# Five columns of gathers taken off GpSimd and fetched row by row by ScalarE and SyncE, with first transfers, last chunk and last wait moved

## The chip, the cores and the metric

One core of one Trainium2 chip. The metric is the device time of the kernel in microseconds, the median of several executions. The kernel is written out by hand: one instruction stream for each engine, with semaphores between them, in four blocks that follow one another.

## What is computed

Two layers of a graph network over 12,500 nodes and 412,500 edges with 64 features; the edges are sorted by their target node dst. Cut to what matters:

```python
edge_index_t = jnp.stack([src, dst], axis=1)
h = jnp.maximum(_layernorm(x), 0.0)
# layer 0: gated MLP of every edge, summed at dst
m = silu(silu(edge @ W1 + b1) @ W2 + b2) * sigmoid(silu(edge @ G1 + g1) @ G2 + g2)
x = x + h + segment_sum(m, dst, n)
# layer 1: attention over the edges of each node
h = jnp.maximum(_layernorm(x), 0.0)
se, re = (h @ Ws + bs)[src], (h @ Wr + br)[dst]
logits = einsum('ehd,d->eh', mish(se + re), aw) + ab
ex = exp(logits - segment_max(logits, dst)[dst])
out = segment_sum(ex / segment_sum(ex, dst)[dst] * se, dst)
x = x + out
```

## The kernel before

**Edge stage** (`edge_mlp`, 202 chunks of 2 x 1024 edges). SyncE loads the edges with features on the partitions (`load`, line 277), TensorE and ScalarE run the gated MLP, VectorE multiplies and forms running sums along the edges with a scan (line 490) that a keep mask restarts at each new node; TensorE turns the sums into rows, and SyncE stores every running sum in DRAM (`sums`). The mask `keep16` comes from comparing neighbours in dst (line 559). It goes to DRAM and comes back spread over partitions (`load_keep`, line 281). A search, spread over the chunks and fed by samples of dst (lines 321 to 335), finds for each node its last edge (`R["last"]`, `R["end"]`) and its first (`R["start"]`), 98 columns of 128 nodes. In program order SyncE issues: edges 0, three pieces of dst, edges 1, the samples, edges 2 and 3, then waits for the mask. ScalarE issues all the first weights (lines 448 to 459). GpSimd's last act is to load x into `R["base"]` in seven pieces (line 667).

**Node update** (`update_nodes`). GpSimd gathers the sum of each node's last edge, 98 indirect DMAs of 128 rows (line 754), one for each column, then scatters 98 columns of projected rows back into `sums` (line 760), a group of seven columns at a time when VectorE has it ready (`sr_ready`). The 14 groups run through: VectorE `center` (line 820), ScalarE Square and Sqrt (`root`, lines 789 and 791), VectorE `scale`, TensorE transposes (777), ScalarE's two copies to `hT` (806), TensorE's projection (782), VectorE's addition to `sr` (846). There are four `sr` buffers; group k waits until the scatters of group k - 4 have landed. On VectorE `project(k - 1)` stands ahead of `spread_of(k)`; on ScalarE `root(k + 1)` stands behind the copies of group k.

**Attention** (`attention`, 135 chunks of up to 24 edges on each of 128 partitions; the last two have 16). GpSimd gathers the senders' rows, a column of 128 at a time (1044). Some columns are not gathered by it: SyncE (line 1000) and ScalarE (line 1112) read node numbers from SBUF into registers (`reg_load`, lines 997 and 1109) and issue one direct DMA for each row. ScalarE computes mish in four activations: Tanh (1081), Square (1087), Ln (1089) and Exp (1095), the last two with a table load each, and the Exp goes to PSUM, where it must wait until the copy of the previous chunk's states (`arows`, line 1156) has left it. VectorE forms the logits (1217 to 1219), the running maximum and the weighted sums by scans. SyncE stores the running states of every edge (`states`, line 984) and waits at the end until all have landed (line 1032).

**Finish** (`finish`). A short chain over VectorE, TensorE and ScalarE joins the states across partitions, GpSimd reads and writes back the rows concerned (1340, 1342), and then gathers the final state of each node, 98 indirect DMAs of 128 rows of 72 values (1347), seven for a group. VectorE divides and adds (1419 to 1427), SyncE stores (1333). Two buffers q; a group waits until the one two before it has been taken.

## Time and profile before

| | us |
|---|---|
| median of 3 runs | 5454.18 (5453.94 to 5455.4) |
| the profiled execution | 5462.94, its span 5461.1 |
| edge stage, node update, attention, finish (start of each) | 0, 1091.0, 1341.2, 5318.3 |
| busy, share of the span | GpSimd 66%, VectorE 79%, ScalarE 53%, TensorE 20% |
| DMA, mean over the span | 115 GB/s; 262 GB/s in most of the edge stage |

Times are microseconds from the start of the span. Busy shares are averages over stages with different limits, so each change is to be read in its own stage. "Idle before, releaser" in square brackets is how long the engine had stood idle before an instruction and what ended that; "issue" means that nothing in the profile held it but its own instruction stream. A name like SPq or ACTq is the queue of an engine, which issues DMAs.

### The profile page before, as it was taken

Reading aid. Unit: us, or ns where it says so; the run is one execution under the profiler, and the core shown is the slowest. Engines: PE = TensorE matmul, PEld = TensorE weight load, DVE = VectorE, ACT = ScalarE, POOL = GpSimd, SP = SyncE. Lnnn points to the kernel's source line nnn. Section 1 sums busy time; section 2 is a strip of 40 time slices with the busy share of each in tenths; the row PEclk is TensorE's granted clock in tenths of the full one; section 3 lists DMA queues with packets and bytes.
Section 4 is the critical chain, followed back from the end, with each engine's and each line's share of the span. In section 5 each row is a group of like instructions: output and inputs, shape, how many; then the busy total and the mean of one; then the engine's idle time right before and its main releaser. Section 6 shows DMA issues by size and latency. Waiting matters only on the chain. (4 is left out here: it accounts for less than half of the span.)

```text
span 5461.1 us, 64454 instructions
## 1 busy us (share of the span) xinstructions
PE 1117.6 (20%) x8383; PEld 509.2 (9%) x8383; DVE 4320.5 (79%) x4065; ACT 2889.7 (53%) x3445; POOL 3594.0 (66%) x3683
## 2 busy tenths in 40 slices
PE   8999999913000000000000000000000000000000
PEld 3444444412000000000000000000000000000000
DVE  7999988753698888888888888888888888888881
ACT  7999999811355445444444444454454454454440
POOL 2444420077777777777777777777777777777757
PEclk9999999955555555555555555555555555555555
DMA  8888888721232333332332332332332332333322
GB/s 229 263 262 262 265 261 266 234 47 58 64 101 77 88 89 78 88 89 77 89 89 76 89 89 77 89 89 76 89 88 77 89 88 78 89 84 81 86 58 50
DMA packets 326140, 630.21 MB, mean 115 GB/s; under 512 B 126683, under 2 KB 130292, under 8 KB 325550
## 3 DMA queue, kind: packets, MB, share of 16 engines
q1 hardware_dynamic: 200862, 501.41, 28.3%
q0 software_dynamic: 117904, 125.12, 12.2%
q14 instruction: 328, 2.69, 0.2%
q10 hardware_dynamic: 7040, 0.89, 0.1%
q8 instruction: 6, 0.10, 0.0%
HBM read 391.97 MB, written 235.04 MB: 115 GB/s over the span
## 5 line engine op out<-in xcount | busy, mean ns | idle before, releaser
L1044 POOL DMA_INDIRECT se<-s_proj,idx x2053 | 1942.2, 946 | 626.3 <-issue 626.0
L1044 POOL DMA_INDIRECT r_se<-s_proj,idx x1026 | 970.7, 946 | 313.1 <-issue 313.1
L1134 ACT ACTIVATE held_ps<-exin 128x96 f32<-128x96 f32 x135 | 34.2, 254 | 1920.5 <-DVE z L1206 1914.7
L1354 PE MATMUL a_ps<-r_ident,r_state 128*4 128x128 f32 x1 | 0.4, 373 | 4001.9 <-DVE drop L1383 4001.9
L490 DVE TENSOR_TENSOR_SCAN sums<-keepb,sums,msg 128x1024 f32<-128x1024 bf16 x201 | 472.6, 2351 | 31.3 <-DVE msg L481 27.4
L1245 DVE TENSOR_TENSOR_SCAN work_ps<-work_ps,wse 128x1632 f32<-128x1632 f32 x135 | 479.1, 3549 | 4.6
L419 ACT ACTIVATE hidden<-h_ps,r_b1g 128x1024 f32<-128x1024 f32 x404 | 460.2, 1139 | 4.6 <-PE h_ps L363 4.6
L1192 DVE TENSOR_TENSOR_SCAN held_ps<-held_ps,rnew 128x1536 f32<-128x1536 f32 x135 | 452.2, 3350 | 4.6
L1206 DVE TENSOR_TENSOR z<-se,held_ps 128x1536 f32<-128x1536 f32 (+1 forms) x90 | 244.9, 2721 | 254.6 <-DMA se<-s_proj,idx 241.1
L374 PE MATMUL v_ps<-hidden,r_w2g 64*64 64x512 f32 x1616 | 438.5, 610 | 17.2 <-issue 1.9
L375 PE MATMUL g_ps<-hidden,r_w2g 64*64 64x512 f32 x1616 | 438.5, 616 | 0.0
L363 PE MATMUL h_ps<-edges,r_w1g 64*64 64x512 f32 x3232 | 433.3, 594 | 20.3 <-DMA r_w1g<-in_L_gnn_G 16.4
L1185 DVE SCALAR_TENSOR_TENSOR rnew<-held_ps,rs 128x1536 f32<-128x1536 f32 x135 | 373.6, 2767 | 60.1 <-DVE nlast L1247 42.2
L630 POOL DMA_INDIRECT nodes<-in_dst,block x102 | 167.4, 1641 | 367.1 <-DVE block L521 335.9
L1354 PEld LDWEIGHTS a_ps<-r_ident,r_state 128*4 128x4 f32 x1 | 0.1, 81 | 4002.2 <-DVE drop L1383 4002.2
L426 ACT ACTIVATE value<-v_ps,b 128x512 f32<-128x512 f32 x404 | 281.6, 697 | 61.6 <-PE v_ps L374 56.1
L1217 DVE SCALAR_TENSOR_TENSOR work_ps<-work_ps,z 128x1536 f32<-128x1536 f32 x135 | 236.1, 1749 | 97.6 <-issue 64.1
L481 DVE SCALAR_TENSOR_TENSOR msg<-gate,value 128x1024 f32<-128x1024 f32 x202 | 246.4, 1220 | 77.5 <-ACT gate L429 76.2
L385 PE MATMUL tr_ps<-r_ident,sums 128*128 128x128 f32 x1616 | 287.5, 301 | 5.2 <-DVE rows L497 4.6
L429 ACT ACTIVATE gate<-g_ps,g 128x512 f32<-128x512 f32 x404 | 281.8, 698 | 0.0
L1156 ACT ACTIVATE arows<-work_ps 128x1632 f32<-128x1632 f32 x135 | 205.5, 1522 | 129.3 <-issue 125.3
L1238 DVE TENSOR_TENSOR wse<-se,held_ps 128x1536 f32<-128x1536 f32 (+1 forms) x90 | 248.7, 2763 | 3.1
(210 smaller groups left out, 4650.4 us busy)
## 6 DMA issues: line engine op xcount, KB each, us to landing
states<-arows SPq DMA_DIRECT2D x133, 864.0 KB
edges<-in_edge_attr SPq DMA_DIRECT2D x202, 512.0 KB, 4.8
sums<-rows SPq DMA_DIRECT2D x402, 256.0 KB
rs<-sums SPq DMA_DIRECT2D x133, 768.0 KB, 5.2
fetched<-s_proj SPq DMA_DIRECT2D x6304, 0.2 KB
keepb<-keep SPq DMA_DIRECT2D x404, 128.0 KB, 3.8
fetched<-s_proj ACTq DMA_DIRECT2D x3040, 0.2 KB
se<-s_proj,idx POOLq DMA_INDIRECT x2053
```

Source lines behind the costliest of these rows:

```text
L363: last = nc.tensor.matmul(h_ps[u][units, s, :], R["w1g1"][feats, units], edges[m][feats, half], start=True, stop=True)
L374: last_v = nc.tensor.matmul(v_ps[out, :], R["w2g2"][0:F, :], hid[0:F, s, :], start=True, stop=True)
L375: last_g = nc.tensor.matmul(g_ps[out, :], R["w2g2"][F:2 * F, :], hid[F:2 * F, s, :], start=True, stop=True)
L385: last = nc.tensor.transpose(tr_ps[:, k, j * P:(j + 1) * P], cols[:, 4 * k + j, :], R["ident"][:, :])
L419: nc.scalar.activation(hidden[u][:, :, :], h_ps[u][:, :, :], ACT.Silu, bias=R["b1g1"][:, :]).then_inc(hidden_ready, 1)
L426: nc.scalar.activation(value[m][:, half], v_ps[:, :], ACT.Silu, bias=b2[:, :]).then_inc(gated, 1)
L429: nc.scalar.activation(gate[m][:, half], g_ps[:, :], ACT.Tanh, scale=0.5, bias=g2[:, :]).then_inc(gated, 1)
L490: nc.vector.tensor_tensor_scan(sums[m][:, :], keepb[m][:, :], msg[m % 2][:, :], carry, ALU.mult, ALU.add).then_inc(scanned, 1)
L1044: pool.indirect_dma_start(out=se[b][:, k, :], out_offset=None, in_=D["s_proj"], in_offset=bass.IndirectOffsetOnAxis(ap=node[:, k:k + 1], a ...
L1185: nc.vector.scalar_tensor_tensor(new, hold, 1.0, rs[b][:, 0:w, :].rearrange("p k f -> p f k"), ALU.subtract, ALU.mult).then_inc(rnew_ready, 1)
L1192: nc.vector.tensor_tensor_scan(held_ps[:, 0:F * w], held_ps[:, 0:F * w], flat(new), 0.0, ALU.mult, ALU.add)\
L1245: do(nc.vector.tensor_tensor_scan(work_ps[:, 0:H * HE * w], work_ps[:, 0:H * HE * w], sums.rearrange("p h e t -> p (h e t)"), 0.0, ALU.mul ...
```

## The change

- Node update: GpSimd gathers 96 columns in place of 98. ScalarE fetches the rows of the last two: 16 pieces (`fetch`) of one register load and 16 direct DMAs each, two pieces behind `root(k + 1)` in each of the steps k = 0 to 7. The last group waits for them. VectorE multiplies the row numbers to byte offsets first.
- Finish: 95 columns gathered in place of 98. Of the last three, ScalarE fetches one (eight pieces, one for each of the first eight groups) and SyncE two (16 pieces), into a buffer of their own. ScalarE takes over the stores of the output from SyncE.
- The five columns of row numbers reach the issuing engines' layout through DRAM: GpSimd writes them (five DMAs) and reads them back (one) at the end of the edge stage.
- First transfers: the second weights and biases are issued by SyncE behind edges 0, no longer by ScalarE. SyncE then waits for all the weights before it issues edges 1 and 2 and only then dst.
- Last chunk of the attention: its Tanh and Square move ahead of the exponentials of the chunk before, its Exp writes to SBUF in place of PSUM and stands ahead of the copy to `arows`; VectorE adds its senders right behind the reduction of the logits.
- Last wait: SyncE no longer waits for the stores of states at the end of the attention; GpSimd does at the start of the finish. Buffers and semaphores outlive the block for that.

```diff
             load(0, 0)
+            sp.dma_start(R["w2g2"][0:F, :], A["L0_gnn_W2"]).then_inc(weights_in, 16)
+            sp.dma_start(R["w2g2"][F:2 * F, :], A["L0_gnn_G2"]).then_inc(weights_in, 16)
+            for k in range(2):
+                rows_k = slice(F * k, F * k + F)
+                sp.dma_start(b2[rows_k, :], column(A["L0_gnn_b2"]), **one).then_inc(weights_in, 16)
+                sp.dma_start(g2[rows_k, :], column(A["L0_gnn_g2"]), **one).then_inc(weights_in, 16)
+            sp.wait_ge(first_in, 16 * FIRST_WEIGHTS)
+            sp.wait_ge(weights_in, 16 * WEIGHTS)
+            load(1, 1)
+            load(2, 2)
...
-            load(1, 1)
...
-            load(2, 2)
...
-            act.dma_start(R["w2g2"][0:F, :], A["L0_gnn_W2"]).then_inc(weights_in, 16)
-            act.dma_start(R["w2g2"][F:2 * F, :], A["L0_gnn_G2"]).then_inc(weights_in, 16)
-            for k in range(2):
-                rows_k = slice(F * k, F * k + F)
-                act.dma_start(b2[rows_k, :], column(A["L0_gnn_b2"]), **slow).then_inc(weights_in, 16)
-                act.dma_start(g2[rows_k, :], column(A["L0_gnn_g2"]), **slow).then_inc(weights_in, 16)
...
-            pool.wait_ge(x_in, 16 * (NS // 2))
+            pool.wait_ge(chain, LAST_KNOWN)
+            for i in range(FAR_LAST + FAR_END):
+                of = R["last"][:, NJ - FAR_LAST + i:NJ - FAR_LAST + i + 1] if i < FAR_LAST else R["end"][:, NJ - FAR_END - FAR_LAST + i:NJ - FAR_END - FAR_LAST + i + 1]
+                pool.dma_start(column(D["far"][i * P:(i + 1) * P]), of, **slow).then_inc(x_in, 16)
+            pool.wait_ge(x_in, 16 * (NS // 2 + FAR_LAST + FAR_END))
+            pool.dma_start(R["far"][:, :, :], D["far"].rearrange("(i g q) -> g i q", g=P // GANG, q=GANG), **slow).then_inc(x_in, 16)
+            pool.wait_ge(x_in, 16 * (NS // 2 + FAR_LAST + FAR_END + 1))
...
         def _(pool):
-            for j in range(NJ):
+            for j in range(NJ - FAR_LAST):
...
+            def fetch(i, g):
...
+                rows_at = [act.alloc_register(f"last_{i}_{g}_{q}") for q in range(GANG)]
+                act.reg_load(rows_at, R["far"][g:g + 1, i, :])
+                for q in range(GANG):
+                    at = act.snap(rows_at[q], donate=True, min_val=0, max_val=(P * RUN - 1) * 4 * F)
+                    act.dma_start(agg[g * GANG + q:g * GANG + q + 1, NJ - FAR_LAST + i, :].bitcast(u8), sums_bytes[:, bass.ds(at, 4 * F)])\
+                        .then_inc(far_agg_in, 16)
...
+            pieces = [(i, g) for i in range(FAR_LAST) for g in range(P // GANG)]
             root(0)
+            act.wait_ge(far_ready, 1)
...
                     root(k + 1)
+                for i, g in pieces[2 * k:2 * k + 2]:
+                    fetch(i, g)
...
         def _(dve):
...
             def center(k):
...
-                dve.wait_ge(agg_in[k], 16 * JB)
+                dve.wait_ge(agg_in[k], 16 * JB if k < NS - 1 else 16 * (JB - FAR_LAST))
+                if k == NS - 1:
+                    dve.wait_ge(far_agg_in, 16 * FAR_LAST * P)
...
+            do(nc.vector.tensor_scalar(R["far"][:, 0:FAR_LAST, :], R["far"][:, 0:FAR_LAST, :], 4 * F, None, ALU.mult))
+            do(nc.vector.tensor_scalar(R["far"][:, FAR_LAST:, :], R["far"][:, FAR_LAST:, :], 4 * ROW, None, ALU.mult))
+            dve.sem_inc(far_ready, 1)
...
-def attention(nc, R, A, D, gathered0):
+def attention(nc, R, A, D, gathered0, state_rows, states_in):
...
-        rows = [sb(f"arows{b}", [P, TA, ROW]) for b in range(B)]
+        rows = state_rows
...
-        stored = [sem(f"astored{b}") for b in range(B)]
+        stored = states_in
...
-            for b in range(B):
-                sp.wait_ge(stored[b], 16 * NI)
...
         def _(pool):
...
-            def mish_head(c, b):
+            def mish_square(c):
...
+            def mish_log(c):
...
+                t = narrow(t1, width(c))
...
+            def mish_tail_in_place(c):
...
+                t = narrow(t1, width(c))
+                act.wait_ge(mish_steps, c * 3 + 3)
+                nc.scalar.activation(t, t, ACT.Exp, scale=-1.0).then_inc(r_ready, 1)
...
-                    mish_tail(c)
+                    crossing = last and b == B - 2
+                    if not (last and b == B - 1):
+                        mish_tail(c)
+                    if crossing:
+                        tanh(c + 1, b1)
+                        mish_square(c + 1)
...
-                    if not (last and b + 1 >= B):
+                    if not last or b + 2 < B:
...
+                    if not last or b + 2 < B:
+                        mish_square(c + 1)
...
-                        mish_head(c + 1, b1)
+                        mish_log(c + 1)
+                    if crossing:
+                        mish_tail_in_place(c + 1)
...
-            mish_head(0, 0)
+            mish_square(0)
+            mish_log(0)
...
-                    mish, lgs, lgs_b, kneg, top, sums = act_ps(w), narrow(lg, w), narrow(lgb, w), narrow(knegf[b], w), narrow(mx[b], w), weighted(w)
+                    mish = narrow(t1, w) if last and b == B - 1 else act_ps(w)
+                    lgs, lgs_b, kneg, top, sums = narrow(lg, w), narrow(lgb, w), narrow(knegf[b], w), narrow(mx[b], w), weighted(w)
...
                     do(nc.vector.tensor_reduce(lgs, mish.rearrange("p (h d) t -> p h t d", h=H), AX, ALU.add))
+                    if last and b == B - 2:
+                        add_senders(at, b + 1)
...
-                    if not (last and b + 1 >= B):
+                    if not last or b + 2 < B:
...
+        def fetch(eng, i, g, rows_at):
...
+            eng.reg_load(rows_at, R["far"][g:g + 1, FAR_LAST + i, :])
+            for q_ in range(GANG):
+                at = eng.snap(rows_at[q_], donate=True, min_val=0, max_val=(P * RUN - 1) * 4 * ROW)
+                eng.dma_start(q_last[g * GANG + q_:g * GANG + q_ + 1, JB - FAR_END + i, :].bitcast(u8), states_bytes[:, bass.ds(at, 4 * ROW)])\
+                    .then_inc(far_q_in, 16)
...
         def _(sp):
-            with sp.Fori(0, NS // 2) as i:
-                for b in range(2):
-                    sp.wait_ge(res_ready, i * 2 + b + 1)
-                    sp.dma_start(out_v[:, bass.ds((i * 2 + b) * JB, JB), :], res[b][:, :, :]).then_inc(out_done[b], 16)
+            sp.wait_ge(mended_out, 16)
+            for i in range(1, FAR_END):
+                for g in range(P // GANG):
+                    fetch(sp, i, g, [sp.alloc_register(f"end_{i}_{g}_{q}") for q in range(GANG)])
...
         def _(pool):
...
+            for b in range(B):
+                pool.wait_ge(states_in[b], 16 * (CA // B))
...
-                for m in range(JB):
-                    pool.indirect_dma_start(out=q[k % 2][:, m, :], out_offset=None, in_=D["states"],
+                for m in range(JB if k < NS - 1 else JB - FAR_END):
+                    into = q[k % 2] if k < NS - 1 else q_last
+                    pool.indirect_dma_start(out=into[:, m, :], out_offset=None, in_=D["states"],
...
+            act.wait_ge(mended_out, 16)
+            fetch(act, 0, 0, [act.alloc_register(f"end_0_0_{q_}") for q_ in range(GANG)])
+            for k in range(NS):
+                act.wait_ge(res_ready, k + 1)
+                act.dma_start(out_v[:, k * JB:(k + 1) * JB, :], res[k % 2][:, :, :]).then_inc(out_done[k % 2], 16)
+                if k + 1 < P // GANG:
+                    fetch(act, 0, k + 1, [act.alloc_register(f"end_0_{k + 1}_{q_}") for q_ in range(GANG)])
...
         def _(dve):
...
-                dve.wait_ge(gathered[b], (k // 2 + 1) * 16 * JB)
-                q_v = q[b][:, :, 0:ABW].rearrange("n j (h e) -> n j h e", h=H)
+                dve.wait_ge(gathered[b], (k // 2 + 1) * 16 * JB - (16 * FAR_END if k == NS - 1 else 0))
+                if k == NS - 1:
+                    dve.wait_ge(far_q_in, 16 * FAR_END * P)
+                q_v = (q[b] if k < NS - 1 else q_last)[:, :, 0:ABW].rearrange("n j (h e) -> n j h e", h=H)
...
-        attention(nc, R, A, D, gathered0)
-        finish(nc, R, A, D, out)
+        states_in = [ctx.enter_context(nc.semaphore(f"states_in{b}")) for b in range(B)]
+        state_rows = [ctx.enter_context(nc.sbuf_tensor(f"arows{b}", [P, TA, ROW], f32)) for b in range(B)]
+        attention(nc, R, A, D, gathered0, state_rows, states_in)
+        finish(nc, R, A, D, out, states_in)
...
```

## Rows read from the trace of the kernel before

**Rows 1.** Timeline: start, us, engine, operation; then, by line: ns min/median/max, first and last start.

```profile
1091.71 1.00 POOL L754 DMA_INDIRECT agg<-sums,r_last  x1 [110.79 <-POOLq L161]
...
L754 POOL DMA_INDIRECT agg<-sums,r_last x98: 941/946/1099, 1091.7 to 1213.7; - x98
...
L760 POOL DMA_INDIRECT sums<-sr,r_start x98: 966/972/1237, 1214.9 to 1339.2; - x98
...
L1347 POOL DMA_INDIRECT q<-states,r_end x98: 941/945/1398, 5329.6 to 5453.9; - x98
```

**Rows 2.** Timeline of the node update: VectorE, ScalarE, then GpSimd.

```profile
1160.00 1.28 DVE L846 TENSOR_TENSOR sr<-pr_ps,r_bsr 128x512 f32<-128x512 f32 x2 [4.01 <-PE pr_ps L782]
...
1170.14 1.28 DVE L846 TENSOR_TENSOR sr<-pr_ps,r_bsr 128x512 f32<-128x512 f32 x2 [4.01 <-PE pr_ps L782]
...
1224.79 1.28 DVE L846 TENSOR_TENSOR sr<-pr_ps,r_bsr 128x512 f32<-128x512 f32 x2 [28.23 <-DMA sums<-sr,r_start]
...
1316.96 1.28 DVE L846 TENSOR_TENSOR sr<-pr_ps,r_bsr 128x512 f32<-128x512 f32 x2 [6.30 <-PE pr_ps L782]
...
1162.09 0.30 ACT L791 ACTIVATE h_std<-h_st,h_eps 128x7 f32<-128x7 f32 x1 [5.10 <-DVE h_st L828]
...
1165.74 0.96 ACT L806 ACTIVATE hT<-hT_ps 64x512 f32<-64x512 f32 x2 [3.35 <-PE hT_ps L777]
...
1214.90 1.01 POOL L760 DMA_INDIRECT sums<-sr,r_start  x1 [0.30 <-issue]
...
1331.57 0.97 POOL L760 DMA_INDIRECT sums<-sr,r_start  x1 [0.30 <-issue]
```

**Rows 3.** Row fetches in the attention stage: SyncE's, then ScalarE's and the activation behind.

```profile
L997 SPq TENSOR_LOAD <-r_picks x394: 1131/1140/4190, 1367.3 to 5132.6; - x197
...
L1000 SPq DMA_DIRECT2D fetched<-s_proj x6304: 224/228/660, 1368.6 to 5138.6; - x197
...
1368.64 31.52 SPq L1000 DMA_DIRECT2D fetched<-s_proj  x80
...
L1112 ACTq DMA_DIRECT2D fetched<-s_proj x24: 213/213/456, 1448.1 to 1457.9; - x24
...
1458.19 1.53 ACT L1156 ACTIVATE arows<-work_ps 128x1632 f32<-128x1632 f32 x1 [8.10 <-issue]
```

**Rows 4.** Timeline of the start of the edge stage.

```profile
4.25 14.00 SPq L277 DMA_DIRECT2D edges<-in_edge_attr  x2
...
16.39 3.69 PE L363 MATMUL h_ps<-edges,r_w1g 64*64 64x512 f32 x16 [16.39 <-DMA r_w1g<-in_L_gnn_G]
...
18.56 3.52 DVE L559 TENSOR_TENSOR r_keep<-dsti 128x3223 bf16<-128x3223 int32 x1
...
39.48 1.63 SPq L277 DMA_DIRECT2D edges<-in_edge_attr  x1
...
42.44 1.99 PE L363 MATMUL h_ps<-edges,r_w1g 64*64 64x512 f32 x8 [3.91 <-DMA edges<-in_edge_attr]
```

**Rows 5.** Timeline of the last chunk of the attention.

```profile
5294.30 0.29 ACT L1141 ACTIVATE arows<-mx 128x64 f32<-128x64 f32 x1
...
5297.94 1.06 ACT L1089 ACTIVATE t<-t 128x1024 f32<-128x1024 f32 x1
...
5298.90 1.06 ACT L1156 ACTIVATE arows<-work_ps 128x1088 f32<-128x1088 f32 x1
...
5300.04 1.28 ACT L1095 ACT_TABLE_LOAD   x1
...
5302.39 1.23 DVE L1217 SCALAR_TENSOR_TENSOR work_ps<-work_ps,z 128x1024 f32<-128x1024 f32 x1 [3.95 <-ACT work_ps L1095]
```

**Rows 6.** Change of stage: SyncE's waits, then the timeline.

```profile
SPq L1032 <- DMA states<-arows: 2.4, 1, 2.4
...
5318.33 0.06 DVE L1381 MEMSET mx_t<- 4x1 f32 x1 [4.13 <-PEq L885]
...
5327.14 1.00 POOL L1342 DMA_INDIRECT states<-fgot,r_mend  x1 [7.26 <-DVE fgot L1413]
```

More of the change, by code:

```diff
@@ L68 @@
 ACT_FIRST = [(0, j, h) for j in range(LEAD) for h in range(SHARE[j] * 2, P // HALF)]
+FAR_LAST, FAR_END = 2, 3
+LAST_KNOWN = 7
 BIG = 1e30
@@ L703, in update_nodes @@
         chain = sem("chain")
+        far_ready = sem("far_ready")
+        far_agg_in = sem("far_agg_in")
         agg_in = [sem(f"agg_in{k}") for k in range(NS)]
@@ L1281, in _, with finish @@
             dve.wait_ge(state_out, 2)
-def finish(nc, R, A, D, out, ABW=F + H):
+def finish(nc, R, A, D, out, states_in, ABW=F + H):
     with ExitStack() as ctx:
@@ L1308, in finish @@
         q = [sb(f"q{b}", [NP, JB, ROW]) for b in range(2)]
+        q_last = sb("q_last", [NP, JB, ROW])
         inv = sb("inv", [NP, JB, H])
@@ L1433, in gnn_program @@
         "samples": nc.dram_tensor("samples", [S1, S2], i32).ap(),
+        "far": nc.dram_tensor("far", [(FAR_LAST + FAR_END) * P], i32).ap(),
         "firsts": nc.dram_tensor("firsts", [S1], i32).ap(),
@@ L1445, in gnn_program @@
             "head": ([P, 1], i32), "mend": ([P, 1], i32), "mcol": ([P, 1], i32), "mhot": ([P, 1], f32), "cont": ([P, 1], f32),
-            "half_state": ([F, P], f32), "picks": ([P // GANG, PICKS, GANG], i32), "se0": ([P, TA, F], f32), "onward": ([P, 1], f32),
+            "half_state": ([F, P], f32), "picks": ([P // GANG, PICKS, GANG], i32), "se0": ([P, TA, F], f32), "far": ([P // GANG, FAR_LAST + FAR_END, GANG], i32), "onward": ([P, 1], f32),
             "whole": ([P, 1], f32), "state": ([P, ROW], f32),
```

3 lines of the change are left out of this document (added).

## The prediction

> **What bounds the kernel now.** I read the page first (engine shares, the slices, the chain that ended last), then the timeline around each place that the diff touches. The kernel is four stages one behind the other: the edge MLP to 1091 us, the node update to 1341, the attention scan to 5318 and the finish to 5461. In the two stages that lose gathers GpSimd issues one indirect DMA after another, 0.95 us of work and 0.30 us between two: the reader is to see that 98 gathers fill 1091.7 to 1213.7, 98 scatters 1214.9 to 1339.2, and 98 gathers of the finish 5329.6 to 5453.9, with nothing but "issue" before them [rows 1]. So a gather taken off that queue is worth 1.26 us (122.0 / 97) in the update and 1.28 us (124.3 / 97) in the finish, as long as GpSimd stays the last to be ready.
>
> In the update it is so by a margin only. Beside GpSimd runs a loop over 14 groups, VectorE, ScalarE's root, VectorE, TensorE, ScalarE's copies to hT, TensorE, VectorE's sr. Its first steps come every 10.14 us (sr at 1160.00 and 1170.14), it then stands still until the first scatters free a buffer (sr at 1224.79) and goes on every 10.24 us to 1316.96 [rows 2]. The last group's sr is complete at 1318.2; GpSimd gets to that group's scatter at 1331.57. The slack is 13.3 us at the end, and 28 us in the pause.
>
> **The row fetches in the update: the large term.** Two gathers go (2 x 1.26 = 2.5 us), and 256 single rows come onto ScalarE's queue: 16 pieces of 16, two behind the root of each of the steps 0 to 7. ScalarE's instructions are in order: the copies to hT of the next step stand behind the 32 DMA issues. That an issue holds up the next activation is shown in the attention stage: 24 row fetches from 1448.1 to 1457.9, and the activation behind them had stood idle 8.10 us on "issue" [rows 3]. The price of a piece: SyncE issues 80 rows in five pieces in 31.52 us, without the first register load of 1.14 us, so (31.52 + 1.14) / 5 = 6.5 us a piece of 16. ScalarE's 24 rows took 9.8 us with their loads of eight registers and without the first; a DMA instruction is 0.213 us there against SyncE's 0.228 [rows 3], 32 x 0.015 = 0.5 us less for two pieces. I take 13.1 - 0.5 = 12.6 us for the 32 rows of a step. Bounds: below, the DMA instructions alone, 32 x 0.213 = 6.8 us; above, ScalarE's own 24 rows in 9.8 + 0.8 us scaled to 32, 14.1 us.
>
> Between the end of the root (1162.09 + 0.30) and the next copies (1165.74) lie 3.35 us in which ScalarE has nothing to do [rows 2]. They hide that much: each of the eight steps gets 12.6 - 3.35 = 9.25 us longer, 19.39 us. VectorE's two new multiplications of the row numbers ahead of everything add an estimated 0.4 us. With sr(0) complete at 1161.28 + 0.4 = 1161.7:
> sr(4) 1239.3, sr(5) 1258.7, sr(6) 1278.0, sr(7) 1297.4, sr(8) 1316.8; behind it nothing is fetched, five more steps of 10.24: sr(13) 1368.0.
> GpSimd starts its scatters at 1212.4, 2.5 us earlier, and needs a new group every 8.97 us (124.3 / 97 x 7): group 4 at 1248.3, ready; group 5 at 1257.2, not ready until 1258.7; from there it waits for each group. Group 13 starts at 1368.0 in place of 1331.57: **+36.4 us**. The earlier start of the scatters and the pause are used up in this sum. With 6.8 us a step the loop stays ahead (sr(13) at 1321.6, wanted at 1329) and the stage is 2.5 us shorter; with 14.1 us it is 48 longer. The value stands near the upper end, because both rows of whole pieces lie there. The far rows land on time: group 13 wants them at some 1350, the last is issued before 1312.
>
> The Trainium skill ("Trainium Kernel Development and Optimization", Key Constraints) says that issuing DMAs from several engines at once only saves the sequencer's issue time, since all run on the same 16 DMA engines. By that rule the move is worth what GpSimd spends on five gathers, about 6.3 us, and costs nothing; the first rival is what comes of it. The traces of rows 3 show the other side of the rule: the issue time is not saved but paid by ScalarE, 128 instructions for one.
>
> **What feeds it.** At the end of the edge stage GpSimd writes five columns to DRAM and reads them back behind its last load of x. It stood idle 110.79 us there [rows 1]; two round trips fit: 0. Should this land late, the bound is some 10 us.
>
> **First transfers.** Now TensorE starts at 16.39 us on its first weights, since these share the DMA engines with dst and three edge loads. The change lets only edges(0) and the weights go first and holds everything else back until they have landed. TensorE will start some 6 to 9 us earlier. That is worth nothing by itself: TensorE stood still again at 42.44 us for 3.91 us, for an edge load that SyncE issued at 39.48 [rows 4], behind the chain dst, keep, samples and firsts; from there the loop runs at its pace and has nothing to catch up with. And dst, issued before at 1.2 us, now goes out behind both waits and two edge loads, at an estimated 8.5. keep started at 18.56, right behind another VectorE instruction, so dst may have been there for some time; and SyncE's fourth edge load hung until 18.25 in a queue that was full, as the queue will be again, later [rows 4]. Of the 7.3 us of delay I count 3, **+3.0 us**; bounds -3.9 (the wait at 42.44 goes) and +7.3.
>
> **Last chunk.** Tanh and Square of the last chunk are moved ahead, so that ScalarE does Ln right behind its copy of mx (ends 5294.59), then Exp in place in SBUF, without the copy to arows between them (1.06 us, at 5298.90). Table load 1.28, Ln 1.06, table load 1.28, Exp 1.03 (from the end of the load at 5301.32 to VectorE's start at 5302.39) [rows 5]: ready at 5299.3 or so in place of 5302.36, and VectorE is done with the chunk before when that copy starts, by 5298.90. **-3.0 us**. VectorE's addition of senders only changes place; ScalarE's exponential now stands behind that Tanh and Square, 2 us by the length of the Ln, which run while VectorE does its small steps. If it came 1 us later, -2.0; the DVE instructions on SBUF in place of PSUM may take 0.2 us either way.
>
> **Last wait.** SyncE waited 2.4 us at the end of the stage for the states to land [rows 6]; GpSimd takes this wait over, and VectorE's chain of the finish, which starts at 5318.33, comes 2.4 us earlier. It needs fgot only near its end; GpSimd had waited 7.26 us for it before the write of the mended rows [rows 6]. The gather starts when the states have landed, about 1 us earlier than now and 2.5 us before it is wanted. **-2.4 us**, bounds -1 and -2.6.
>
> **Three gathers of the finish.** 3 x 1.28 = **-3.8 us**, if the rows are there. SyncE issues 256 rows in 16 pieces of 6.5 us, 105 us from the write of the mended rows; it ends 15 us before GpSimd's last gather. ScalarE has one piece (6.3 us) a group of 8.97 us, with the output's DMA ahead of it. Both are hidden. If the pieces took 7.5 us, SyncE would end with GpSimd; each 0.5 us more costs 8 us.
>
> **Sum.** 36.4 + 3.0 - 3.0 - 2.4 - 3.8 = +30.2 us. The profiled execution took 5462.94 us with a span of 5461.1; it would become 5493.1. The median of the three runs, 5454.18, lies 8.8 below it; the same difference gives 5484.4 us, 0.55% slower.
>
> **Rivals.**
> 1. Faster: ScalarE's fetches stay hidden in the update. The mechanism is the slack of four sr buffers, 28 us of pause and 13.3 us at the end: it decides the sign at 8.8 us a step (15.6 us from sr to sr), where group 13 comes 6.2 us late and the rest gives 6.2 back. For it: the pause is real. Against it: whole pieces of 16 at 6.5 us. Then -2.5 + 3.0 - 3.0 - 2.4 - 3.8 = -8.7: 5445.5. 8%.
> 2. The start gains as meant: -3.9 in place of +3.0, all else as forecast: 5477.5. For it: keep may have waited for VectorE, not for dst. Against it: SyncE issues 7 us later whatever feeds the late edge load. 15%.
> 3. SyncE's rows bound the finish, at 8 us a piece: 5329.4 - 5.4 + 128 + 2.4 puts the last row at 5454.4 on the old clock, where the last gather would have landed 9.2 us before the old 5456.5: +7.1, 5491.5. For it: single register loads up to 4.2 us occur in the loop; against: 16 pieces average them out. 5%.
> 4. The change as forecast, 5484.4: 72%; its own range is 5473 to 5497.
>
> The range of 8 in 10 reaches from 5464 (shorter pieces, 10.9 us a step, with the start's gain of 3.9) to 5501 (14.1 us a step and dst 7.3 us late). A difference below 0.2%, 11 us, counts as no change. Faster by more asks rival 1 together with a gain at the start: 3%. No change is rival 1 by itself and the lower tail: 9%. Slower: 88%.
>
> **What would show it.** In the profile after: sr of the update some 19 us apart for eight steps and 10.2 for five; "hT" on ScalarE waiting for issue by 9 us eight times; GpSimd waiting for sr before its scatters from group 5 on, which it never did; the update from 1091 to about 1378. The first matrix product before 10 us, but the same pause before the edge load, at 44 to 47 us. The last chunk's first VectorE step 3 us earlier against the chunk before; 5.4 us less from the last z to the first gather of the finish; 95 gathers, and the last group ready at GpSimd's landing, not at a row's. I am wrong if a step with two pieces takes less than 15 us, or if GpSimd's scatters keep their pace.

## The result, and the profile after

| | before | after |
|---|---|---|
| median, us | 5454.18 (5453.29 to 5455.4, 5 runs) | 5503.01 (5502.27 to 5505.97, 5 runs) |
| profiled execution, its span | 5462.94, 5461.1 | 5502.27, 5500.4 |
| edge stage | 1091.1 | 1101.7 |
| node update | 251.6 | 295.5 |
| attention | 3975.6 | 3965.0 |
| finish | 142.8 | 138.2 |

The ratio is 1.0090, 95% interval 1.0079 to 1.0102: 48.8 us slower. The prediction had the direction, and the update's mechanism and place. It forecast 30.2 us, 18.6 too few, and the time lies 2 us above its range of 5464 to 5501. Stages are counted between VectorE's memsets that open them.

The four stages of the two profiled executions differ by +10.6, +43.9, -10.6 and -4.6, which is +39.3 and not +48.8, because the profiled execution of before ran 8.8 us above its own median. Where that lies is seen in v3 below, a run that leaves the attention as it was: it shows 3970.6 us for it, and 944 ns for a mean gather of the senders, where the profile before has 3975.6 and 946. The profile of v2, which leaves the attention as it was too and also ran 9.9 us above its median, has 3977.8 and 947. So some 5 of attention's 10.6 us belong to that one execution, and 5.6 to the change.

The node update, VectorE's additions to `sr` in order of time (start, us, operation, idle before and its releaser); the counterpart in [rows 2] came every 10.14 us:

```profile
1170.96 1.28 DVE L874 TENSOR_TENSOR sr<-pr_ps,r_bsr 128x512 f32<-128x512 f32 x2 [4.36 <-PE pr_ps L795]
1191.14 1.28 DVE L874 TENSOR_TENSOR sr<-pr_ps,r_bsr 128x512 f32<-128x512 f32 x2 [14.02 <-PE pr_ps L795]
...
1333.26 1.28 DVE L874 TENSOR_TENSOR sr<-pr_ps,r_bsr 128x512 f32<-128x512 f32 x2 [14.35 <-PE pr_ps L795]
1343.50 1.28 DVE L874 TENSOR_TENSOR sr<-pr_ps,r_bsr 128x512 f32<-128x512 f32 x2 [4.10 <-PE pr_ps L795]
...
1384.46 1.28 DVE L874 TENSOR_TENSOR sr<-pr_ps,r_bsr 128x512 f32<-128x512 f32 x2 [6.30 <-PE pr_ps L795]
```

(1333.26 - 1170.96) / 8 = 20.3 us a step while rows are fetched, 10.24 behind them. The view names TensorE as what VectorE waited for, but TensorE was late itself. Who was late is seen on ScalarE, in the same timeline:

```profile
1173.05 0.30 ACT L804 ACTIVATE h_std<-h_st,h_eps 128x7 f32<-128x7 f32 x1 [5.10 <-DVE h_st L856]
1175.02 11.61 ACTq L820 DMA_DIRECT2D agg<-sums  x32
1186.73 0.96 ACT L830 ACTIVATE hT<-hT_ps 64x512 f32<-64x512 f32 x2 [13.38 <-issue]
```

The copy to hT stood 13.38 us on "issue" where it had waited 3.35 us for TensorE [rows 2]. Where the 13.4 go, from the groups of ScalarE's queue (ns min/median/max):

```profile
L817 ACTq TENSOR_LOAD <-r_far x16: 1286/1558/1866, 1173.1 to 1322.2; - x16
```

```profile
L820 ACTq DMA_DIRECT2D agg<-sums x256: 217/217/503, 1175.0 to 1328.4; - x128
```

The 11.61 us of the row above hold 32 rows and the second of two register loads. So there are two loads of 16 words at 1.56 us, and (11.61 - 1.56) / 2 = 5.0 us for each 16 rows: 13.2. GpSimd's scatters then wait for `sr`, which they never did before, where 0.30 us of issue is all that stood between two [rows 2]. The first wait is at group 5 (1273.69), and from the next group on they wait for the whole difference of the two loops, 20.3 less 8.97 us (GpSimd's timeline):

```profile
1273.69 0.97 POOL L773 DMA_INDIRECT sums<-sr,r_start  x1 [6.99 <-DVEq L876]
...
1294.17 0.97 POOL L773 DMA_INDIRECT sums<-sr,r_start  x1 [11.55 <-DVEq L876]
...
1334.88 0.97 POOL L773 DMA_INDIRECT sums<-sr,r_start  x1 [11.57 <-DVEq L876]
...
1386.08 0.96 POOL L773 DMA_INDIRECT sums<-sr,r_start  x1 [1.63 <-DVEq L876]
```

The start of the edge stage, which answers to [rows 4]: TensorE begins 8.5 us earlier and stops for edge loads at 15.15 and 27.65 instead; VectorE's comparison for the keep mask waits for dst alone and starts 5.60 us later.

```profile
7.88 3.26 PE L373 MATMUL h_ps<-edges,r_w1g 64*64 64x512 f32 x16 [7.88 <-DMA r_w1g<-in_L_gnn_G]
8.25 0.83 SPq L279 DMA_DIRECT2D edges<-in_edge_attr  x2
9.13 1.23 SPq L329 DMA_DIRECT2D dsti<-in_dst  x1
...
15.15 1.09 PE L373 MATMUL h_ps<-edges,r_w1g 64*64 64x512 f32 x8 [1.44 <-DMA edges<-in_edge_attr]
24.16 3.52 DVE L563 TENSOR_TENSOR r_keep<-dsti 128x3223 bf16<-128x3223 int32 x1 [15.26 <-DMA dsti<-in_dst]
...
27.65 1.99 PE L373 MATMUL h_ps<-edges,r_w1g 64*64 64x512 f32 x8 [2.86 <-DMA edges<-in_edge_attr]
```

In before, the comparison stood behind VectorE's own wait for the last of the weights, and dst was there by the time it came to it:

```profile
17.82 0.15 DVE L552 TENSOR_SCALAR g<-g 128x1 f32<-128x1 f32 x1 [16.66 <-DMA g<-in_L_gnn_g]
```

The running sums of chunk n, counted from 0, begin 5.2 us later than before at n = 3 and 4.4 at n = 183. From 183 to 184 that jumps to 10.8, and it stays at 10.5. There GpSimd prepares the five columns (its timeline):

```profile
984.81 0.54 POOL L671 DMA_DIRECT2D r_base<-in_x  x1 [25.26 <-DVE sums L494]
985.34 1.07 POOL L675 DMA_DIRECT2D far<-r_last  x2
986.40 1.59 POOL L675 DMA_DIRECT2D far<-r_end  x3
1001.60 0.63 POOL L677 DMA_DIRECT2D r_far<-far  x1 [13.61 <-DMA far<-r_end]
```

The last chunk, which answers to [rows 5] and [rows 6] (ScalarE and VectorE, in order of time):

```profile
5343.05 0.29 ACT L1185 ACTIVATE arows<-mx 128x64 f32<-128x64 f32 x1
5343.36 1.28 ACT L1122 ACT_TABLE_LOAD   x1
...
5347.02 1.06 ACT L1134 ACTIVATE t<-t 128x1024 f32<-128x1024 f32 x1
...
5348.11 1.23 DVE L1267 SCALAR_TENSOR_TENSOR t<-t,z 128x1024 f32<-128x1024 f32 x1 [0.95 <-ACT t L1134]
...
5350.63 1.86 DVE L1269 TENSOR_REDUCE lg<-t 128x64 f32<-128x1024 f32 x1
...
5360.22 1.08 ACT L1204 ACTIVATE arows<-work_ps 128x1088 f32<-128x1088 f32 x1 [3.92 <-DVEq L1300]
...
5362.20 0.06 DVE L1454 MEMSET mx_t<- 4x1 f32 x1 [1.66 <-PEq L916]
```

From the copy of mx to VectorE's start are 5.06 us, where before took 8.09 [rows 5]. In the profile before, the reduction and the last copy to arows were these, and the finish started at 5318.33 [rows 6]:

```profile
5304.93 1.22 DVE L1219 TENSOR_REDUCE lg<-work_ps 128x64 f32<-128x1024 f32 x1
...
5313.88 1.08 ACT L1156 ACTIVATE arows<-work_ps 128x1088 f32<-128x1088 f32 x1 [3.92 <-DVEq L1248]
```

So the reduction of the same 128x1024 values takes 0.64 us more where it reads SBUF (1.86) than where it read PSUM (1.22), the last copy to arows starts 12.11 us behind VectorE's first step (before 11.49), and the finish starts 1.98 us behind that copy (before 4.45).

### The profile page after: what moved, and what is told of

It is laid out like the page before. It is cut to its first block and busy times, and to the rows that moved or that the text cites. A ratio compares the mean times of both kernels' runs of the same rounds, so it can differ in the third digit from the quotient of the medians.

```text
span 5500.4 us, 65723 instructions
## 1 busy us (share of the span) xinstructions
PE 1120.8 (20%) x8383; PEld 509.7 (9%) x8383; DVE 4321.0 (79%) x4067; ACT 2889.4 (53%) x3445; POOL 3587.7 (65%) x3684
```

## The experiments

What was open: whether the update's loss is ScalarE's queue or the rows themselves, and what the start and the preparation cost each. Twelve runs (e, s, t, w) were taken while before itself had a median of 7162 to 7176 us. This is called the long condition below. In it the engines' instructions are as long as here, but the engines stand idle longer, more often on "issue" and "remote" (released by nothing that the profile of this core shows), and 256 rows issued by SyncE take 181 to 183 us and not 105. It is no property of a chip: chip 8 showed 7161.69 for before beside t1 and 5454.29 beside u1. Each ratio is against before taken beside it; u ran where before takes 5454.29, v where it takes 5455.78.

**Before, one look (e0).**

> The kernel before, profiled once more. The two profiles shown so far differ by 39.3 us in span, the medians by 48.8. Theory: the profiled execution of before was a slow one on GpSimd (mean 946 ns an indirect DMA against 944 in the profile after, over 3079 of them 5.7 us, and the attention drifts by 5.7 us with the same instructions); then this profile has a span near 5452 and its attention stage is some 5 us shorter than 3977. Rival: the attention stage of the changed kernel is faster by itself; then this profile repeats 5461 and 3977.

7160.91 us, against 7176.31 of the runs beside it: the first sign of the long condition. Its stages (edge 1121.8, update 298.0, attention 5591.6, finish 148.2) are what the e, s, t and w runs are read against. Its own question, whether the changed kernel's attention is faster by itself, it can't answer; the 3970.6 us of v3, given above, answer it for the theory: the profiled execution of before was slow on GpSimd.

**The change again, and with half the rows (u1, u2).** u2 is after with

```diff
-FAR_LAST, FAR_END = 2, 3
+FAR_LAST, FAR_END = 1, 3
...
-                for i, g in pieces[2 * k:2 * k + 2]:
+                for i, g in pieces[k:k + 1]:
```

> The kernel after, unchanged, on a chip on which before takes about 7165 us and an engine pays more for every instruction that it issues without work of its own (there 16 row fetches of ScalarE take 12 to 15 us, of SyncE some 20 us). Theory: the price of the change is ScalarE's issue time, so it grows with that: 32 rows a step at 24 to 28 us in place of 13.5, sr 30 to 34 us apart for eight steps, the update 400 to 450 us in place of before's 298; with SyncE's rows also setting the end of the finish (+50), in all 7330 to 7390. Rival: what costs in the update is the transfers, not their issue; then the update is some 340 us as on the first chip (before plus 44) and the whole 7270 to 7280.

> The kernel after with one column in place of two fetched by ScalarE in the update: eight pieces of 16 rows, one a step; GpSimd gathers 97. Theory: the cost goes by the issue time left over behind ScalarE's 3.35 us of slack a step, 16 rows being 12 to 14 us on such a chip: sr 19 to 21 us apart for eight steps, the update 330 to 350 us, 7265 to 7290 in all. On the first chip the same count, 6.5 us less 3.35 = 3.3 us a step, would stay inside the slack of the four sr buffers and cost nothing. Rival: half the rows, half of after's loss, wherever the line crosses the slack.

u1 took 5505.03 us, ratio 1.0089 (1.0074 to 1.0105), update 295.6: the result again. u2 took 5454.09, ratio 1.0 (0.9991 to 1.0009), update 251.2. Both expectations had been written for the long condition, and u1's question, whether the price grows with the issue time, was not put to the test. What u2's says of the first chip, that one piece costs nothing, is what came. Of ScalarE and VectorE in u2:

```profile
1170.35 0.30 ACT L804 ACTIVATE h_std<-h_st,h_eps 128x7 f32<-128x7 f32 x1 [5.10 <-DVE h_st L856]
1172.34 5.13 ACTq L820 DMA_DIRECT2D agg<-sums  x16
1177.57 0.96 ACT L830 ACTIVATE hT<-hT_ps 64x512 f32<-64x512 f32 x2 [6.92 <-issue]
```

```profile
1231.13 1.28 DVE L874 TENSOR_TENSOR sr<-pr_ps,r_bsr 128x512 f32<-128x512 f32 x2 [15.82 <-DMA sums<-sr,r_start]
1244.90 1.28 DVE L874 TENSOR_TENSOR sr<-pr_ps,r_bsr 128x512 f32<-128x512 f32 x2 [7.63 <-PE pr_ps L795]
```

The step is 13.8 us, longer than GpSimd's 8.97 too, but the pause before sr(4) still exists (15.82 us) and GpSimd first waits at group 12 (0.71 us). Half the rows lose none of the 44 us, not half of them: the rival of proportion falls. The slack of four `sr` buffers takes what one piece adds and not what two add, and with 0.71 and 1.63 us of waiting at the last two groups it is about used up.

**No rows on ScalarE (e3, s3, w3: one kernel).** After with GpSimd gathering 98 columns in the update, ScalarE fetching nothing:

```diff
-            for j in range(NJ - FAR_LAST):
+            for j in range(NJ):
...
-                for i, g in pieces[2 * k:2 * k + 2]:
-                    fetch(i, g)
```

> The changed kernel with ScalarE's row fetches of the node update taken out and GpSimd gathering all 98 columns again; all else stays. Theory: the fetches are the whole loss of that stage, its loop goes back from 20.3 to 10.2 us a step and the stage from 295.2 to 250.7 us + 0.4 for the two multiplications: -44, 5459. Rival: part of the stage's loss is VectorE's new work or the later start; then the stage stays above 253 us and the time above 5462.

> The kernel after with the row fetches of ScalarE in the node update taken out and GpSimd gathering all 98 columns again; the preparation, the first transfers, the last chunk, the last wait and the finish are those of after. Theory: the whole loss of the update is the 32 row fetches a step on ScalarE; without them the update takes its old 250 us and the kernel is +4.8 (start) +6 (preparation) -5 (last chunk and wait) -3.8 to -4.6 (finish) = about +2 against before, 5456. Rival: ScalarE's fetches explain only the 36 us of the prediction and the rest sits elsewhere in the update (register loads, numbers multiplied, landing of the last group), then the kernel is 5462 to 5466.

> The kernel after with no row fetches in the update, GpSimd gathers 98 columns (as s3). Theory: update 251.5, in all 2.5 above w2: 5459 to 5462. That is the whole of after but for ScalarE's fetches: start +5.4, preparation +7.3, tail -3.7, finish -4.6, sum +4.4. Rival: preparation and start overlap, each hidden in part behind the other, and their sum is under 10: 5455.

Ratios 1.0086 (1.0072 to 1.01), 1.0088 (1.0074 to 1.0102) and 1.0082 (1.0068 to 1.0096): 58 to 61 us slower, in the long condition. The update was 296.5 to 298.0 against the 298.0 of e0, as the theory wanted, and the rival that wanted more falls; but after itself was never run in this condition, so its update there is not known. The whole came out otherwise, mainly because of the finish, 198.5 to 200.3 for 148.2. The expectation had left out that there a row costs SyncE 0.7 us on average. SyncE's queue in w3:

```profile
7040.08 180.67 SPq L1384 DMA_DIRECT2D q_last<-states  x256
```

GpSimd's 95 gathers were through in 141 us there. Most rows go out as fast as in after: 173 of the 255 intervals between two are under 0.4 us (235 in after). The rest of the time is 62 pauses of 0.7 to 3.5 us within the pieces, whose cause was not looked into. This is rival 3 of the prediction, found in the long condition only.

**The rows on SyncE (w2, t1: one kernel).** After with `fetch` moved to SyncE, eight pieces ahead of its loop of stores of s_tab, one behind each of the first eight stores.

> The kernel after with one thing changed: the 256 single rows of the node update are issued by SyncE (eight pieces ahead of its store loop, one piece behind each of its stores of s_tab in the first eight steps), not by ScalarE. On a chip where before takes 5454: theory (ScalarE's queue is what costs, 32 rows a step ahead of its copies to hT): the update takes 249 us in place of after's 295, sr comes every 10.2 us, GpSimd never waits for sr; the kernel is at after minus 46 = about 5457, that is +3 against before (start +5, preparation +6, one gather less by two -2.5, last chunk and wait -5). Rival: the rows themselves cost, whoever issues them (single-row transfers beside GpSimd's scatters, or the last group's rows landing late): the update stays above 270 us and the kernel above 5480.

> The kernel after with the 256 rows of the update issued by SyncE, not ScalarE (as t1). Theory: the update is 249.5 in place of 295.5, GpSimd never waits for sr; 46 below after, 5457 to 5459, with start and preparation still paid (5.4 and 7.3 by v3 and v2). Rival, the rows themselves cost: update above 270, kernel above 5480.

Ratios 1.01 (1.0085 to 1.0115) and 1.0101 (1.0085 to 1.0116), updates 312.4 and 312.0, against the 298.0 of w3, which ran beside w2: not free. In t1, `sr` shows who waits (VectorE):

```profile
1342.22 1.28 DVE L876 TENSOR_TENSOR sr<-pr_ps,r_bsr 128x512 f32<-128x512 f32 x2 [24.27 <-DMA s_proj<-sr]
```

The stores of s_tab stand behind 128 rows in SyncE's queue, and the `sr` buffers stay taken until they have landed. In this condition neither theory is settled by the total; the next kernel shows the same move where before takes 5455.78.

**A version made from the findings (v1, s4: one kernel; w1).** First transfers as before; the row numbers brought over by SyncE inside the update; rows on SyncE as in w2; last chunk, last wait and finish of after.

```diff
+            sp.dma_start(rows_d[:, 0:FAR_LAST], R["last"][:, NJ - FAR_LAST:NJ], allow_slow_non_contiguous=True).then_inc(far_in, 16)
+            sp.dma_start(rows_d[:, FAR_LAST:], R["end"][:, NJ - FAR_END:NJ], allow_slow_non_contiguous=True).then_inc(far_in, 16)
...
+                sp.reg_load(rows_at, R["far"][g:g + 1, :, i])
...
+            for i, g in pieces[0:8]:
+                fetch(i, g)
             for k in range(NS):
...
+                for i, g in pieces[8 + k:9 + k]:
+                    fetch(i, g)
```

> A version made from the findings: first transfers as before; the row numbers of the five columns are brought over by SyncE inside the node update (two writes and one read of 128 and 8 pieces, no longer 640 single elements) while GpSimd gathers; the 256 rows of the update are issued by SyncE, which has nothing else to do there (eight pieces ahead of its store loop, one behind each of its stores of s_tab); last chunk, last wait and finish as in after. Theory: the update keeps its pace and loses two gathers (-2.5), last chunk and wait -5, finish -3.8: -11 us, 5443. Rival: the mere presence of 256 single-row transfers beside GpSimd's gathers costs, whoever issues them (the loop of the update or GpSimd's scatters slow down): over 5454.

> The same version as s4 (first transfers as before, the row numbers brought over inside the node update in few pieces, the update's rows on SyncE, last chunk, last wait and finish as in after), meant for a chip where before takes 5454 and a piece of 16 rows 6.5 us. Theory: with SyncE's issue time hidden the update keeps 251 us or loses the two gathers, sr never waits for a row: update 249 to 251, attention as with the last chunk alone (3965), finish 138: -3.7 (last chunk and wait as measured) -4.6 -2.5 = -11, 5443 to 5445. Rival: the eight pieces ahead of SyncE's first store of s_tab (52 us) hold up the first four sr buffers and with them the loop; then the update is 5 to 20 us longer and the kernel at 5450 to 5465.

v1: 5468.13 us, ratio 1.0023 (1.0014 to 1.0032): slower than before by 12.3. The stages: edge 1090.3, update 249.5, attention 3965.3, finish 161.4. Three of four are what the theory wanted: on SyncE the 256 rows cost the update nothing, and it is 2.05 us shorter than before. VectorE waited 30.93 us for a store of s_tab before sr(4), 2.7 us more than the pause that it had anyway (28.23 [rows 2]), and GpSimd never waited for `sr`. So it is not the rows that cost, but their place in ScalarE's queue. The finish failed by the layout of the row numbers: the tile held the five numbers of a node side by side, so that a register load read 16 words 20 bytes apart. The groups of its loads, and for comparison those of after's finish, where the words are neighbours:

```profile
L1386 SPq TENSOR_LOAD <-r_far x16: 3446/3614/4230, 5316.2 to 5452.2; - x16
```

```profile
L1385 SPq TENSOR_LOAD <-r_far x16: 1136/1232/1658, 5373.3 to 5472.9; - x16
```

SyncE's 16 pieces take 16 x 2.4 = 38 us longer. In after their last row was issued 15 us ahead of GpSimd's last gather, so 23 of the 38 show in the finish (161.4 for 138.2), and VectorE's last group waits for the rows:

```profile
5462.14 0.33 DVE L1495 RECIPROCAL inv<-q_last 128x28 f32<-128x28 f32 x1 [27.93 <-DMA q_last<-states]
```

w1 is v1 with the row numbers landing in a tile of their own, `farin`, from which VectorE's multiplication writes neighbours into `far`; the loads then read 16 neighbours. Nothing else changed (the multiplication, one of two):

```diff
-            do(nc.vector.tensor_scalar(R["far"][:, :, 0:FAR_LAST], R["far"][:, :, 0:FAR_LAST], 4 * F, None, ALU.mult))
+            do(nc.vector.tensor_scalar(R["far"][:, 0:FAR_LAST, :], R["farin"][:, :, 0:FAR_LAST].rearrange("g q i -> g i q"), 4 * F, None, ALU.mult))
```

> v1 with one change: VectorE's multiplication writes the row numbers out in the order in which they are read, so that a register load reads 16 neighbouring words and no longer 16 words that lie 20 bytes apart. Theory: v1's register loads took 3.4 to 4.2 us each, 16 of them on SyncE put its last row 23 us behind GpSimd's gathers; contiguous they take 1.1, the finish is 138 us in place of 161.4, the update stays at 249.5, and the kernel is 23 below v1: 5445, 10 below before. Rival: SyncE's rows are slow for another reason (two engines on the same transfers); then the finish stays above 150 and the kernel above 5457.

It was taken in the long condition: ratio 1.0088 (1.0074 to 1.0101), where s4, which is v1 in that condition, had 1.0134 (1.0119 to 1.015). The loads in the finish fell from 3.5 to 1.23 us, update and finish from 329.7 and 211.8 to 313.9 and 201.4. That the stride costs is shown; that the version beats before is not, and in the long condition it is slower than before. v1's first three stages with after's finish of 138.2 would give a span of 5443.3, by estimate some 11 us under before; w1 was not run where before takes 5455.78.

**The preparation alone (v2, s2, e2) and the first transfers alone (v3, s1, e1).** Before with the one or the other part of the change's diff added.

> Before, with the preparation of the five columns of row numbers alone (GpSimd writes them to DRAM and reads them back at the end of the edge stage; nobody uses them). Theory: 640 elements of 4 bytes written and read back hold up the stores of sums, and VectorE and TensorE wait once: +6 us, 5460 (in the profile after the scans jump from +4.4 to +10.5 us there). Rival, the step of the prediction: GpSimd stood idle there, cost 0, 5454.

> The kernel before with only the preparation of the five columns of row numbers added (five writes and one read, 640 elements of 4 bytes each way, by GpSimd at the end of the edge stage); nobody uses them. Theory: the one-element transfers fill the 16 DMA engines' queues, a store of sums waits behind them, TensorE and VectorE stop once, and the scan of the chunks from 183 on is 6 us late: 5460, node update from 1097. Rival, the prediction's term: two round trips fit into GpSimd's idle time and cost nothing, 5454, node update from 1091.

> The kernel before with only the preparation of the five columns added (as s2). Theory: 640 single elements of 4 bytes each way fill the DMA queues while SyncE stores sums; the edge loop stops once: +6, 5460, node update from 1095 to 1097. Rival, the prediction's term: hidden, 0, 5454, from 1089 to 1091.

> Before, with the first transfers of the change alone (SyncE issues the second weights, waits for all weights, then edges 1 and 2, then dst). Theory: dst and the samples go out 8 us later, the chain to the late edge load moves with them, and this costs +4.5 to +5 us (the scans of the profile after lie 5.15 us late from the fourth on): 5459. Rival (what the prediction took, +3): 5457. Rival, the gain of an earlier first matrix product: -4, 5450.

> The kernel before with the first transfers of the change alone (second weights and biases on SyncE, SyncE waits for all the weights, then edges 1 and 2, then dst). Theory: what sets the loop is the chain dst, keep mask, samples, edge load 5 on SyncE, which comes 4 to 5.5 us later; the loop over chunks never catches up, so the kernel is 4.5 to 5 us longer (about 5459). Rival A, the prediction's term: +3.0 (5457.2). Rival B, the wait at 42 us goes: -3.9 (5450.3). In the profile: start of the node update at 1095.5 to 1096 in place of 1091.1.

> The kernel before with only the first transfers of the change (as s1). Theory: dst goes out 7 us later behind the weights, and keep, samples and edge load 5 follow by 4 to 5: +4.5, 5459. Rival, the prediction's: +3.0; the other end that it gave: -3.9, 5450.

v2: 5463.06 us, ratio 1.0013 (1.0004 to 1.0022), +7.3, of which the interval makes +2 to +12. v3: 5461.14, ratio 1.001 (1.0001 to 1.0019), +5.4, by the interval +0.5 to +10.4. The preparation's rival, no cost, falls. For the start the interval holds the theory's 4.5 and the prediction's 3.0 alike; there the rows decide, since the sums of v3 run 5.1 us behind before's from chunk 3 on and 4.5 at the end. In the long condition the totals (1.0004 and 1.0005 for the preparation, 1.0001 and 1.0002 for the start, each 0.0009 either way) neither show nor exclude these costs. In v2 the chunks' sums run 0.2 us behind before's up to chunk 183 and 6.6 from 186 on. Its timeline there (DVE and ACT wait for a store of sums, TensorE for edges):

```profile
996.18 1.98 PE L365 MATMUL h_ps<-edges,r_w1g 64*64 64x512 f32 x8 [2.69 <-DMA edges<-in_edge_attr]
997.76 0.63 POOL L675 DMA_DIRECT2D r_far<-far  x1 [14.01 <-DMA far<-r_end]
998.39 0.60 ACT L437 ACTIVATE rows<-tr_ps 128x512 f32<-128x512 f32 x1 [3.59 <-DMA sums<-rows]
998.39 0.69 DVE L499 COPY rows<-tr_ps 128x512 f32<-128x512 f32 x1 [7.67 <-DMA sums<-rows]
```

And v2 by windows of 15 us (busy of PE, PEld, DVE, ACT, POOL, then granted clock, DMA share, GB/s); the writes of 640 elements are issued at 981 and waited for until 998:

```profile
975.00:990.00 15.00, 14.80 (x120) 6.51 (x116) 12.04 (x10) 14.11 (x22) 3.20 (x6) 1.00 0.89 208
990.00:1005.00 15.00, 11.19 (x72) 3.96 (x68) 6.86 (x7) 8.52 (x12) 0.63 (x1) 0.77 0.98 258
```

The same two windows in before:

```profile
975.00:990.00 15.00, 14.78 (x119) 6.33 (x113) 12.04 (x10) 14.12 (x22) 0.54 (x1) 1.00 0.83 265
990.00:1005.00 15.00, 14.78 (x119) 6.35 (x112) 11.48 (x10) 14.13 (x21) 0.00 (x0) 1.00 0.80 258
```

The round trips fit into GpSimd's idle time, as predicted, and yet cost: the DMA engines were 80 to 83% busy with the edge loop's own transfers already. With the 640 elements beside them the share rises to 0.89 and 0.98, and no more is moved for it (208 and 258 GB/s for 265 and 258).

How much the preparation costs varies, as the profiled executions show, one for each run. The sums fall back by 6.4 us in v2, 6.1 in after and 8.7 in u1 around chunk 184, and by only 0.8 in u2, which has one column fewer: four writes of 128 elements, and GpSimd waits 9.7 us for them and not 13.6. One execution of each can't tell how much of that is the missing column.

In v3, the comparison for the keep mask shows the start's mechanism:

```profile
23.94 3.52 DVE L561 TENSOR_TENSOR r_keep<-dsti 128x3223 bf16<-128x3223 int32 x1 [15.38 <-DMA dsti<-in_dst]
```

**The last chunk and the last wait alone (u3).** Before with these two parts.

> The kernel before with the last chunk and the last wait of the change alone. Theory: the exponential of the last chunk runs in SBUF ahead of the copy to arows and the finish's chain no longer waits for the states to land: -3.0 and -2.4, 5 to 5.5 us less, of 7165 a ratio of 0.9993, at the edge of what five rounds tell; in the profile the time from the end of ScalarE's last copy to arows to the finish's first VectorE instruction is 2.0 us in place of 4.45, and the last chunk's first step on VectorE stands some 3 us nearer to the chunk before. Rival: the gather of the states in the finish waits for the same stores, so the last wait only moves and gives 0: -3.

5450.62 us, ratio 0.9993 (0.9984 to 1.0002), -3.7; the interval does not exclude that there is no effect. Its rows are those of after: VectorE starts 5.07 us behind the copy of mx, the finish 1.98 us behind the last copy. By rows the two parts are worth -3.03 + 0.62 = -2.4 and -2.5. The gather of the states starts 2.71 us into the finish and is waited for by nobody new (the first gather of a column starts 11.3 us into the finish in before, after and u3 alike), so the rival falls.

**The sum.** Update +43.9 (profile), preparation +7.3 (v2), start +5.4 (v3), last chunk and wait -4.9 (rows), finish -4.6 (profile): +47.1, measured +48.8. The two terms of v2 and v3 are known to some 5 us each. In u2 the same terms with the update at -0.4 would give +2.8, and -0.2 was measured, 4.9 us either way; its small loss around chunk 184 is on the side of that difference.

## Where the prediction was right, and where it fell 18.6 us short

Two steps of the sum failed. The term for the row fetches in the update, +36.4, was mis-sized: it measured +43.9. The term for what feeds them, 0, left out the DMA engines' side: it measured +7.3. These are 14.8 of the 18.6 us; the start's 2.4 make most of the rest. In the order of the prediction:

- **The row fetches in the update: right in mechanism and place, mis-sized.** Predicted were 12.6 us and 19.39 a step, +36.4; measured were 13.4 and 20.3, +43.9. Eight steps of 0.9 us more are 7.2 of the 7.5. The register loads are what was priced too low: at SyncE's 1.14 us [rows 3], where ScalarE's took 1.56, two a step, 2 x 0.42 = 0.84 us. The rows themselves came out a little cheaper (2 x 5.0 us for 2 x 5.15), and the small gaps around the loads and rows, some 0.3 us, stood in no term. A load of 16 words on ScalarE stood in no row of before; ScalarE's own loads of eight took 0.73 there. The Trainium skill ("DMA: Bandwidth & Descriptors", Latency and other measured facts) gives a register load a floor of about 0.6 us; the trace agrees, with 0.73 for eight words and 1.56 for sixteen. The upper bound of 14.1, from ScalarE's own rows, held the value. GpSimd first waited at group 5, as predicted. The prediction's remark that a cheap step keeps the loop ahead is what u2 shows (13.8 us a step, no loss). The Trainium skill ("DMA: Bandwidth & Descriptors", Issuing engines are not separate DMA queues) calls the time to initiate a DMA usually small beside the DMA itself; here the issues of 32 rows and a load held ScalarE for 11.6 us in each step, and the prediction's rival by which such issues stay hidden fell for two pieces a step.
- **What feeds it: wrong, the step whose mechanism failed.** "Two round trips fit: 0" counted GpSimd's time. The price, 7.3 us, fell on the DMA engines, and through them on the stores of sums and an edge load. The table of before already gave 262 GB/s for that stretch. The bound of "some 10" was for arriving late, which did not happen. v2 shows that the preparation costs. What it is about the 640 elements that costs, their number or their place in the queues, was not tried by itself; u2's 0.8 us with 512 elements points at the number, but is one execution.
- **First transfers: right in sign, +5.4 for +3.0.** Of an estimated 7.3 us by which dst goes out later the prediction counted 3, on the guess that dst had lain ready for some time before 18.56. It had landed by then, since VectorE did not wait for it, but how long before, no view shows. In after it goes out 7.9 us later (9.13 for 1.2), and the comparison, which now waits for it, starts 5.6 us later: only 2.3 us of the delay are hidden. The samples, firsts and the edge load behind follow. The wait of TensorE at 42.44 did not go: in after it ends at 47.48, after 4.06 us.
- **Last chunk: -2.4 for -3.0.** VectorE's start came 3.03 us nearer, as worked out; the reduction on SBUF gave 0.64 back. The prediction had allowed 0.2 for SBUF.
- **Last wait: -2.5 for -2.4**, and the finish had room for the gather.
- **Three gathers of the finish: -4.6 for -3.8.** SyncE's 16 pieces took 104.8 us for the 105 predicted. Here the rows are in time; at 3.6 us a load (v1) or in the long condition they set the end.
- **Rival 1** (hidden in the slack) was sound as a mechanism: it is what happens with one piece a step. Its threshold of 15.6 us a step lies between the 13.8 of u2, which lost nothing, and the 20.3 of after, and was not tried itself.

## What to carry to other kernels

Here, taking an indirect DMA off GpSimd saved 1.25 us and cost another engine's queue about 53 us for its 128 rows; that is worth it only on a queue with nothing behind it that a loop needs, and the register load is part of the price, word layout included. A loop with buffers between it and the bottleneck does not pay in proportion: work out the step at which the slack ends, and stay below it. A transfer whose issuing engine is idle is not free by that: v2's cost 7.3 us where the DMA engines were 80 to 83% busy. So read the DMA share of the window as well as the idle time of the engine that issues it.

## What was not expected of the hardware

- A register load of 16 words takes 1.2 us on SyncE and 1.5 on ScalarE if they are neighbours, and 3.6 and 3.9 if they lie 20 bytes apart (v1).
- 640 elements of 4 bytes, written in five DMAs, kept GpSimd waiting 14 us for their landing and stopped the edge loop for 6.4 (v2). TensorE stood still for 2.69 us there, until 996.18. Its granted clock was 1.00 (2.4 GHz) up to 994, 0.50 (1.2 GHz) from 996 to 1002, and 1.00 again from 1004; the window's 0.77 is the mean over both levels.
- At times the same program takes 7162 to 7176 us with the same busy durations. Most of it is the attention, 5591.6 us for 3975.6; SyncE's 256 rows take 181 us for 105, the finish of before 148.2 for 142.8, the update 298 for 252. What slows the issue was not looked into.
